# Graph passes with seven and ten row buffers, three one-hot buffers, and table rows stored bank by bank

## The chip, the core and the metric

The kernel runs on one core of one Trainium2 chip. The metric is the device time of one execution in microseconds (us); of the kernel before there are three timed runs and one profiled execution. The engines are TensorE (PE; its weight loads are listed as PEld), VectorE (DVE), ScalarE (ACT), GpSimd (POOL) and SyncE (SP), which only issues transfers.

## What is computed

Four graph layers over 3125 nodes with 256 features and 53125 edges, each followed by a layer norm: a filter layer, an attention layer, a three-step mean aggregation, and two relational convolutions. The change touches the last two. Cut to what matters:

```python
# layer 3 (L2): three times
agg = segment_sum(h[src], dst) / deg
h = relu(agg @ W_agg[l] + h @ W_self[l] + b_hid[l])
# then h @ W_out + b_out, residual and layer norm
# layer 4 (L3): two convolutions with relu between
xb  = einsum('ni,bio->nbo', x, basis)            # 4 bases
msg = einsum('eb,ebo->eo', comp[edge_type], xb[src])
agg = segment_sum(msg * norm[key][:, None], dst)
out = agg + x @ root + bias
```

## The kernel before

The edges were sorted at the start of the kernel. They lie in NT = 440 tiles of 128 edges; four tiles (U = 4) are a **group**, so that a pass has 110 groups. The nodes are NB = 25 blocks of 128. A **pass** goes over all edges once:

- GpSimd gathers, for each tile, 128 rows of 1 KB from a table in HBM into a row buffer (`rows`). It does so with one indirect transfer per tile, four per group, and before it reuses a buffer it waits on the semaphore `summed`, until the group that had the buffer has been summed.
- VectorE builds the one-hot matrices of a group (`hot`, 128x512), one operation, or two where edges have weights.
- TensorE multiplies one-hot by rows (each f32 product stands in the profile as two matmuls of 128x256, so a group is eight) and adds into one of four PSUM banks, one increment of `summed` for each tile. It waits for the rows (`gathered`) and for `hotted`.
- ScalarE fills a bank for a block (`fill`) and drains it (L1491) when the block's last tile is summed.

There are five passes. Four are made by `fused_pass`: two of the mean aggregation that also make the next table with 256 columns (the first and the second pass here), a third that has a projection and a layer norm in between (`measure`) and makes a table with 8 x 256 = 2048 columns, `rel_table`, and a fourth that makes the second `rel_table`. The fifth is made by `aggregate_pass`, which only sums. The code of `fused_pass` is straight line: the class `Posts` says after which group a finished block is turned (TensorE transposes, L1437; VectorE copies, `keep`, L1517) and, one group later, multiplied by the next layer's weights (`product`, L1451; VectorE takes the result out of PSUM in `take`, L1551, one copy for each 512-column bank plus one for the part that stays in SBUF). VectorE works in order: at step n it makes the one-hot of group n + 2 (AHEAD = 2), and then what `Posts` asks for after group n.

All buffers are rings. `g.RING` = 5 is the number of row buffers and of one-hot buffers in all five passes. The rows of the next table stand in two buffers `o` of all the columns; SP stores a buffer with one transfer when all its banks have been taken, and VectorE waits in `take` for the store of two blocks before (`stored`).

The two waits on which the passes turn are, on GpSimd and on VectorE:

```python
if n >= ring:
    pool.wait_ge(summed, (n - ring + 1) * U + 1)     # L1415, L1248
...
if n >= ring:
    dve.wait_ge(summed, (n - ring + 1) * U + 1)      # L1504
```

Between two passes all engines meet at a barrier, after the last store has landed.

## Time and profile before

| | us |
|---|---|
| median of three timed runs | 8323.25 (8320.33 to 8326.89) |
| the profiled execution's own time | 8298.08 |
| its span, first to last instruction | 8296.4 |
| first pass, 4961 to 5604 | 643 |
| second pass, 5604 to 6246 | 642 |
| third pass (with projection), 6246 to 6957 | 711 |
| fourth pass, 6957 to 7627 | 670 |
| fifth pass (sums only), 7627 to 8262 | 635 |

The five passes are 3301 us of the span. Everything before 4961 us is as it was, and so is what comes behind the fifth pass.

How to read it: an engine's busy time is a share of its stretch. "Idle" before an instruction is put down to whatever released it last by the profile; where the named one is a transfer that had ended long before (here "DMA table<-p_o" or "DMA bias<-bias_parts"), the wait belongs to another semaphore of the same instruction. "issue" is idle time for which the profile shows no wait. On GpSimd an idle time of 0.30 us before each gather is the rule.

### The profile page before, as it was taken

What the parts mean: (1) busy time and instruction counts of PE and PEld (TensorE: products, weight loads), DVE (VectorE), ACT (ScalarE), POOL (GpSimd) and SP (SyncE); (2) the same over time, 40 slices, a digit from 0 to 9 for tenths busy, and PEclk for the clock granted to TensorE, in tenths of its full rate; (3) what the DMA queues carried; (4) which work ended last, traced back from release to release, by engine and by line L of the source; (5) the groups of instructions that cost most, each with busy time, mean ns of one, the idle gap of its engine ahead of it and who ended that gap; (6) DMA issues with size and microseconds to landing.
All of it is one profiled execution on the core that took longest, in us unless ns stands there. A gap on an engine that the chain in (4) does not pass through costs nothing. (4 is left out here: it accounts for less than half of the span.)

```text
span 8296.4 us, 76731 instructions
## 1 busy us (share of the span) xinstructions
PE 5016.2 (60%) x19899; PEld 3266.6 (39%) x19900; DVE 3362.9 (41%) x7405; ACT 1335.8 (16%) x3186; POOL 4680.3 (56%) x4578
## 2 busy tenths in 40 slices
PE   1675754726633555555688885555556786776554
PEld 1342432414422333333465764433434454444333
DVE  8335346302212666666788432111213443333222
ACT  0332321300212222222222540000000000000000
POOL 3565754662364666566344216666665664665765
PEclk7786876857766565566799997776777887888666
DMA  2232321215204555455343013333333333444333
GB/s 81 83 99 67 99 81 58 90 42 170 96 22 129 165 161 162 151 160 161 116 121 109 14 36 97 98 92 104 99 97 106 129 128 102 131 129 114 94 91 89
DMA packets 413034, 865.48 MB, mean 104 GB/s; under 512 B 87540, under 2 KB 248707, under 8 KB 406326
## 3 DMA queue, kind: packets, MB, share of 16 engines
q0 software_dynamic: 216368, 576.59, 24.0%
q1 hardware_dynamic: 196486, 286.70, 10.3%
q8 instruction: 87, 1.43, 0.1%
q14 instruction: 93, 0.76, 0.0%
HBM read 664.47 MB, written 198.58 MB: 104 GB/s over the span
## 5 line engine op out<-in xcount | busy, mean ns | idle before, releaser
L1419 POOL DMA_INDIRECT p_rows<-table,idx_s x1320 | 1282.9, 972 | 776.8 <-issue 372.1
L1463 PE MATMUL p_psA<-p_rows,p_hot 128*128 128x256 f32 x3520 | 1044.6, 454 | 556.1 <-DMA p_rows<-table,idx_s 219.9
L1463 PEld LDWEIGHTS p_psA<-p_rows,p_hot 128*128 128x128 f32 x3520 | 779.6, 229 | 772.9 <-issue 644.8
L1768 DVE TENSOR_REDUCE p_best<-p_psM 128x8 f32<-128x1024 f32 x440 | 537.3, 1221 | 541.5 <-remote 351.8
L520 POOL DMA_INDIRECT rec_s<-p_space,p_row_s x416 | 452.5, 1088 | 519.8 <-DVE p_space L717 400.0
L1667 POOL DMA_INDIRECT p_kg<-kv_table,p_at x440 | 455.9, 1036 | 465.2 <-ACT p_at L1631 346.0
L1684 PE MATMUL p_psM<-ident,p_cold 128*128 128x512 bf16 x880 | 417.6, 573 | 378.1 <-DVE p_best L1768 259.5
L755 POOL DMA_INDIRECT rec_d<-edge_d,norm x416 | 399.7, 961 | 401.3 <-POOLq L76 271.9
L592 PE MATMUL p_psW<-p_wf,p_hid 128*128 128x256 f32 x1664 | 596.1, 492 | 0.0
L1419 POOL DMA_INDIRECT p_rows<-rel_table,edge_d x440 | 431.8, 981 | 267.7 <-issue 123.8
L512 POOL DMA_INDIRECT p_space<-h_table,at_d x416 | 442.3, 1063 | 209.0 <-issue 126.5
L1252 POOL DMA_INDIRECT p_rows<-rel_table,edge_d x440 | 439.9, 1000 | 210.6 <-issue 126.7
L1551 DVE COPY p_o<-p_psO 128x512 f32<-128x512 f32 (+1 forms) x250 | 158.1, 638 | 958.0 <-remote 497.9
L1667 POOL DMA_INDIRECT p_qg<-q_table,p_at x440 | 440.0, 1000 | 140.4 <-issue 140.4
L1267 PE MATMUL p_psA<-p_rows,p_hot 128*128 128x256 f32 x880 | 344.4, 553 | 288.7 <-DMA p_rows<-rel_table,edge_d 215.7
L1687 PEld LDWEIGHTS p_psM<-p_splitT,choose 96*128 96x128 bf16 x3520 | 371.5, 138 | 214.7 <-issue 194.5
L717 DVE SCALAR_TENSOR_TENSOR p_space<-p_psW,p_space 128x256 f32<-128x256 f32 x416 | 172.6, 477 | 697.4 <-remote 325.3
L1687 PE MATMUL p_psM<-p_splitT,choose 96*128 96x128 bf16 x3520 | 417.3, 290 | 0.0
L592 PEld LDWEIGHTS p_psW<-p_wf,p_hid 128*128 128x128 f32 x1664 | 350.7, 234 | 103.5 <-issue 30.4
L1852 POOL TENSOR_TENSOR p_val<-p_val 128x1024 f32<-128x1024 f32 x110 | 210.3, 1911 | 318.2 <-ACT p_val L1841 314.6
L1267 PEld LDWEIGHTS p_psA<-p_rows,p_hot 128*128 128x128 f32 x880 | 226.2, 272 | 407.1 <-issue 368.2
L805 PE MATMUL p_psA<-p_msg,p_hot 128*128 128x257 f32 x880 | 244.6, 418 | 211.4 <-issue 197.0
(316 smaller groups left out, 8252.7 us busy)
## 6 DMA issues: line engine op xcount, KB each, us to landing
p_msg<-rec_s SPq DMA_DIRECT2D x110, 520.0 KB
v_sorted<-p_kg SPq DMA_DIRECT2D x110, 512.0 KB
p_val<-v_sorted SPq DMA_DIRECT2D x110, 512.0 KB
rel_table<-p_o SPq DMA_DIRECT2D x50, 1024.0 KB
p_rows<-table,idx_s POOLq DMA_INDIRECT x1320
p_rows<-rel_table,edge_d POOLq DMA_INDIRECT x880
p_att<-edge_attr SPq DMA_DIRECT2D x104, 127.0 KB
table<-p_o SPq DMA_DIRECT2D x75, 128.0 KB
```

The lines of the kernel that those rows point to most:

```text
L512: pool.indirect_dma_start(msg[q][:, u, 0:D], None, table, bass.IndirectOffsetOnAxis(ap=g.at_d[:, n * U + u:n * U + u + 1], axis=0))\
L520: pool.indirect_dma_start(g.rec_s_rows, bass.IndirectOffsetOnAxis(ap=row_s[:, n * U + u:n * U + u + 1], axis=0), msg[q][:, u, :], None).th ...
L592: step = pe.matmul(psW[:, u, :], hid[t.q % few][:, k, u * P:(u + 1) * P], wf2[:, k, :], start=False, stop=(k == KT - 1))
L755: pool.indirect_dma_start(g.rec_d_rows, bass.IndirectOffsetOnAxis(ap=g.row_d[:, j:j + 1], axis=0), g.rec_all[:, j, :], None).then_inc(plac ...
L1252: pool.indirect_dma_start(rows[q][:, u, :], None, table, bass.IndirectOffsetOnAxis(ap=idx(n * U + u), axis=0))\
L1267: pe.matmul(psA[:, bass.ds(step[u], D)], hot[t.q][:, u, :], rows[t.q][:, u, :], start=False, stop=True, skip_group_check=True).then_inc(su ...
L1419: pool.indirect_dma_start(rows[q][:, u, :], None, table, bass.IndirectOffsetOnAxis(ap=idx(n * U + u), axis=0))\
L1463: pe.matmul(psA[:, bass.ds(step[u], D)], hot[q][:, u, :], rows[q][:, u, :], start=False, stop=True, skip_group_check=True).then_inc(summed, 1)
L1667: pool.indirect_dma_start(rows[t.q][:, u, :], None, table, bass.IndirectOffsetOnAxis(ap=at[t.q][:, u, n:n + 1], axis=0))\
L1684: pe.matmul(psM[u % 2][:, h:h + 4, :].rearrange("p h e -> p (h e)"), cold[t.q][:, u, :], g.ident4[:, :], start=True, stop=False)
L1687: step = pe.matmul(psM[u % 2][:, h, :], choose[:, u * H + h, :], splitT[t.q][:, :], start=False, stop=(h % 4 == 3))
L1768: dve.tensor_reduce(best[:, u, :], psM[u % 2][:, :, :], X, ALU.max).then_inc(found[u], 1)
```

## The change

It has three parts.

1. The number of row buffers is 7 in the four fused passes (`g.ROWS`) and 10 in the fifth (`g.LASTS`), where it was 5.
2. The number of one-hot buffers is 3 in the fused passes (`g.HOTS`); it stays 5 in the fifth.
3. The rows of the next table go through four buffers of one bank each (512 columns, or 256 in the first two passes) and not through two of all columns. SP stores each bank when it has been taken, and VectorE waits before each bank for the store of four banks ago.

```diff
 def aggregate_pass(...)
-    NT, NB, groups, ring = g.NT, g.NB, g.NT // U, g.RING
+    NT, NB, groups, ring = g.NT, g.NB, g.NT // U, g.LASTS
+    hots = g.RING
...
-        hot = [s.sb(f"hot{q}", [P, U, P]) for q in range(ring)]
+        hot = [s.sb(f"hot{q}", [P, U, P]) for q in range(hots)]
...
-                    wait(dve, summed, after(t, ring))
+                    wait(dve, summed, after(t, hots))
...
 class Spread
+        self.sent = [bank[0][0:2] for bank in self.banks if not bank[0][2]]
...
 def fused_pass(...)
-    NT, NB, groups, ring = g.NT, g.NB, g.NT // U, g.RING
-    AHEAD, TURNS, OUTS, OUTB = 2, 3, 2, 3
+    NT, NB, groups, ring, hots = g.NT, g.NB, g.NT // U, g.ROWS, g.HOTS
+    AHEAD, TURNS, OUTS, OUTB = 2, 3, 4, 3
...
-        o = [s.sb(f"o{q}", [P, spread.cols]) for q in range(OUTS)]
+        o = [s.sb(f"o{q}", [P, min(BANK, spread.cols)]) for q in range(OUTS)]
...
-                    sp.wait_ge(taken, posts.made[Posts.SPREAD, k])
-                    sp.dma_start(spread.table[bass.ds(b * P, P), :], o[k % OUTS][:, :]).then_inc(stored[k % OUTS], 16)
+                    for j, (c0, c1) in enumerate(spread.sent):
+                        i = k * len(spread.sent) + j
+                        sp.wait_ge(taken, posts.made[Posts.SPREAD, k] - len(spread.banks) + j + 1)
+                        sp.dma_start(spread.table[bass.ds(b * P, P), c0:c1], o[i % OUTS][:, :]).then_inc(stored[i % OUTS], 16)
...
-                    q, c = n % ring, slice(n * U, (n + 1) * U)
-                    if n >= ring:
-                        dve.wait_ge(summed, (n - ring + 1) * U + 1)
+                    q, c = n % hots, slice(n * U, (n + 1) * U)
+                    if n >= hots:
+                        dve.wait_ge(summed, (n - hots + 1) * U + 1)
...
-                    if k >= OUTS:
-                        dve.wait_ge(stored[k % OUTS], 16 * (k // OUTS))
                     for j, bank in enumerate(spread.banks):
                         last = posts.made[Posts.SPREAD, k] - len(spread.banks) + j
+                        i = k * len(spread.sent) + j
+                        if i >= OUTS and j < len(spread.sent):
+                            dve.wait_ge(stored[i % OUTS], 16 * (i // OUTS))
...
-    g.RING = 5
+    g.RING, g.ROWS, g.HOTS, g.LASTS = 5, 7, 3, 10
```

The order of the work on TensorE, ScalarE and GpSimd stays. On SP, the stores of two blocks of the third pass were these; `rel_table0` is the table that the pass makes, `o0` and `o1` are the two buffers of all columns, and the loads of `order_s` fetch the block's number:

```order
L1408 ISA
L1408 DMA rel_table0<-p17_o0 128x2048
L159 TENSOR_LOAD order_s
L1408 ISA
L1408 DMA rel_table0<-p17_o1 128x2048
```

and the stores of one block are now these:

```order
L1413 ISA
L1413 DMA rel_table0<-p17_o0 128x512
L1413 ISA
L1413 DMA rel_table0<-p17_o1 128x512
L1413 ISA
L1413 DMA rel_table0<-p17_o2 128x512
L1413 ISA
L1413 DMA rel_table0<-p17_o3 128x512
```

One transfer of 1024 KB behind one wait has become four of 256 KB, each behind a wait of its own (the rows named ISA).

On GpSimd, the gathers of the fifth pass went over five buffers. Here is where it comes back to the first of them; a name in brackets is that of a semaphore's first user, and both names stand for `summed` here:

```order
L1252 DMA p19_rows3<-rel_table1,edge_d 128x256 x4
L1252 DMA p19_rows4<-rel_table1,edge_d 128x256 x4
L1252 DMA p19_rows0<-rel_table1,edge_d 128x256 [waits p1_filled]
L1252 DMA p19_rows0<-rel_table1,edge_d 128x256 x3
L1252 DMA p19_rows1<-rel_table1,edge_d 128x256 [waits p1_filled]
```

The same place is now:

```order
L1253 DMA p19_rows7<-rel_table1,edge_d 128x256 x4
L1253 DMA p19_rows8<-rel_table1,edge_d 128x256 x4
L1253 DMA p19_rows9<-rel_table1,edge_d 128x256 x4
L1253 DMA p19_rows0<-rel_table1,edge_d 128x256 [waits p1_bias_in]
L1253 DMA p19_rows0<-rel_table1,edge_d 128x256 x3
```

GpSimd's first wait on `summed` moves from the sixth group to the eleventh, and in each later group it asks for the sums of ten groups before, not of five.

## Rows read from the trace of the kernel before

**Rows 1.** The five passes by window: length, busy time by engine, clock, DMA.

```profile
core 0: us, PE busy (x) PEld busy (x) DVE busy (x) ACT busy (x) POOL busy (x), PEclk, DMA share, GB/s
4961.00:5604.00 643.00, 348.94 (x1159) 255.86 (x1159) 118.17 (x217) 23.58 (x50) 428.01 (x440) 0.76 0.35 98
...
6246.00:6957.00 711.00, 542.45 (x1636) 337.30 (x1637) 272.48 (x786) 23.54 (x50) 426.18 (x441) 0.84 0.38 119
6957.00:7627.00 670.00, 468.60 (x1460) 290.05 (x1459) 232.56 (x371) 19.27 (x50) 431.77 (x440) 0.84 0.42 126
7627.00:8262.00 635.00, 345.68 (x883) 226.36 (x881) 147.90 (x220) 19.02 (x50) 439.91 (x440) 0.71 0.33 91
```

**Rows 2.** GpSimd's waits in the first pass: us in total, times, longest.

```profile
POOL p_rows L1419 <- issue: 124.6, 407, 0.6
...
POOL p_rows L1419 <- DMA table<-p_o: 51.1, 16, 5.3
POOL p_rows L1419 <- PE p_psA L1463: 18.0, 16, 4.7
```

**Rows 3.** The same in the fifth pass.

```profile
POOL p_rows L1252 <- issue: 126.7, 416, 0.3
POOL p_rows L1252 <- PE p_psA L1267: 42.6, 20, 5.4
...
POOL p_rows L1252 <- DMA table<-p_o: 14.6, 3, 5.2
```

**Rows 4.** Fifth pass, GpSimd in order of time: start, us, idle before.

```profile
7774.77 1.40 POOL L1252 DMA_INDIRECT p_rows<-rel_table,edge_d  x1 [4.86 <-DMA table<-p_o]
...
7819.95 0.94 POOL L1252 DMA_INDIRECT p_rows<-rel_table,edge_d  x1 [0.30 <-issue]
7826.04 1.41 POOL L1252 DMA_INDIRECT p_rows<-rel_table,edge_d  x1 [5.15 <-DMA table<-p_o]
```

**Rows 5.** Fifth pass, the same stretch, TensorE's sums of single groups.

```profile
7792.64 1.99 PE L1267 MATMUL p_psA<-p_rows,p_hot 128*128 128x256 f32 x8 [1.22 <-DMA p_rows<-rel_table,edge_d]
7797.69 3.42 PE L1267 MATMUL p_psA<-p_rows,p_hot 128*128 128x256 f32 x8 [3.06 <-DMA p_rows<-rel_table,edge_d]
7802.74 1.99 PE L1267 MATMUL p_psA<-p_rows,p_hot 128*128 128x256 f32 x8 [1.63 <-DMA p_rows<-rel_table,edge_d]
```

**Rows 6.** Fifth pass, the same stretch, VectorE's one-hots.

```profile
7794.80 0.69 DVE L1295 TENSOR_TENSOR p_hot<-iota,edge_d 128x512 f32<-128x512 f32 x1 [1.68 <-PE p_psA L1267]
...
7809.12 0.69 DVE L1295 TENSOR_TENSOR p_hot<-iota,edge_d 128x512 f32<-128x512 f32 x1 [12.80 <-issue]
...
7825.93 0.69 DVE L1295 TENSOR_TENSOR p_hot<-iota,edge_d 128x512 f32<-128x512 f32 x1 [15.27 <-DMA table<-p_o]
```

**Rows 7.** First pass, all engines around one stop.

```profile
5108.28 2.01 PE L1451 MATMUL p_psO<-w_hid,p_xT 128*128 128x256 f32 x4
...
5121.93 0.95 POOL L1419 DMA_INDIRECT p_rows<-table,idx_s  x1 [0.30 <-issue]
5126.24 0.42 DVE L1551 COPY p_o<-p_psO 128x256 f32<-128x256 f32 x1 [18.68 <-remote]
5126.57 0.94 POOL L1419 DMA_INDIRECT p_rows<-table,idx_s  x1 [3.70 <-DMA table<-p_o]
...
5126.91 2.49 DVE L1505 TENSOR_TENSOR p_hot<-iota,loc_s 128x512 f32<-128x512 f32 x4
5127.78 4.63 PE L1463 MATMUL p_psA<-p_rows,p_hot 128*128 128x256 f32 x10 [13.23 <-DVE p_hot L1505]
```

**Rows 8.** Fourth pass, all engines around its first stop.

```profile
6991.55 0.38 PE L1437 MATMUL p_psT<-ident,sums 128*128 128x128 f32 x2
...
7006.80 0.94 POOL L1419 DMA_INDIRECT p_rows<-rel_table,edge_d  x1 [0.30 <-issue]
7013.35 0.42 DVE L1517 COPY p_xT<-p_psT 128x256 f32<-128x256 f32 x1 [34.53 <-DMA bias<-bias_parts]
...
7013.55 0.94 POOL L1419 DMA_INDIRECT p_rows<-rel_table,edge_d  x1 [5.80 <-DMA table<-p_o]
...
7013.83 10.10 PE L1451 MATMUL p_psO<-big,p_xT 128*128 128x512 f32 x16 [16.50 <-DVE p_xT L1517]
```

**Rows 9.** Third pass, around one stop: TensorE's sums end as GpSimd goes on.

```profile
6426.34 3.62 PE L1463 MATMUL p_psA<-p_rows,p_hot 128*128 128x256 f32 x16
...
6428.51 0.94 POOL L1419 DMA_INDIRECT p_rows<-table,idx_s  x1 [4.30 <-PE p_psA L1463]
```

**Rows 10.** VectorE's waits in the fourth pass: us in total, times, longest.

```profile
DVE p_xT L1517 <- DMA bias<-bias_parts: 198.6, 15, 34.5
DVE p_o L1551 <- PE p_psO L1451: 116.5, 67, 7.5
```

**Rows 11.** SP's last stores of the fourth pass, and the fifth pass's first one-hot.

```profile
7607.78 13.70 SPq L1408 DMA_DIRECT2D rel_table<-p_o  x2
...
7626.39 0.69 DVE L1295 TENSOR_TENSOR p_hot<-iota,edge_d 128x512 f32<-128x512 f32 x1 [5.43 <-PEq L76]
```

More of the change, by code:

```diff
@@ L1266, in total @@
                     for u in range(U):
-                        pe.matmul(psA[:, bass.ds(step[u], D)], hot[t.q][:, u, :], rows[t.q][:, u, :],
+                        pe.matmul(psA[:, bass.ds(step[u], D)], hot[t.q % hots][:, u, :], rows[t.q][:, u, :],
                                   start=False, stop=True, skip_group_check=True).then_inc(summed, 1)
@@ L1293, in make_hot @@
                     c = bass.ds(t.n * U, U)
-                    wait(dve, summed, after(t, ring))
-                    dve.tensor_tensor(hot[t.q][:, :, :], bc(g.iota[:, :], 1, U), bc(loc[:, c], 2, P), ALU.is_equal)\
+                    wait(dve, summed, after(t, hots))
+                    dve.tensor_tensor(hot[t.q % hots][:, :, :], bc(g.iota[:, :], 1, U), bc(loc[:, c], 2, P), ALU.is_equal)\
                         .then_inc(marked, 1)
                     dve.wait_ge(marked, t.n + 1)
-                    dve.tensor_tensor(hot[t.q][:, :, :], hot[t.q][:, :, :], bc(weight[:, c], 2, P), ALU.mult).then_inc(hotted, 1)
+                    dve.tensor_tensor(hot[t.q % hots][:, :, :], hot[t.q % hots][:, :, :], bc(weight[:, c], 2, P), ALU.mult).then_inc(hotted, 1)
                 pipelined(dve, groups, ring, [(0, make_hot)])
@@ L1379, in fused_pass @@
         rows = [s.sb(f"rows{q}", [P, U, D]) for q in range(ring)]
-        hot = [s.sb(f"hot{q}", [P, U, P]) for q in range(ring)]
+        hot = [s.sb(f"hot{q}", [P, U, P]) for q in range(hots)]
         xT = [s.sb(f"xT{q}", [P, KT, P]) for q in range(TURNS)]
-        o = [s.sb(f"o{q}", [P, spread.cols]) for q in range(OUTS)]
+        o = [s.sb(f"o{q}", [P, min(BANK, spread.cols)]) for q in range(OUTS)]
         stats, bits, part_f = s.sb("stats", [P, 6]), s.sb("bits", [P, 1], I32), s.sb("part", [P, 1])
@@ L1406, in _ @@
                     b = block_of_rank(core.nc, g, plan, SPE, k)
-                    sp.wait_ge(taken, posts.made[Posts.SPREAD, k])
-                    sp.dma_start(spread.table[bass.ds(b * P, P), :], o[k % OUTS][:, :]).then_inc(stored[k % OUTS], 16)
+                    for j, (c0, c1) in enumerate(spread.sent):
+                        i = k * len(spread.sent) + j
+                        sp.wait_ge(taken, posts.made[Posts.SPREAD, k] - len(spread.banks) + j + 1)
+                        sp.dma_start(spread.table[bass.ds(b * P, P), c0:c1], o[i % OUTS][:, :]).then_inc(stored[i % OUTS], 16)
                 for q in range(OUTS):
-                    sp.wait_ge(stored[q], 16 * len(range(q, NB, OUTS)))
+                    sp.wait_ge(stored[q], 16 * len(range(q, NB * len(spread.sent), OUTS)))
             @block.gpsimd
@@ L1462, in _ @@
                         for u in range(U):
-                            pe.matmul(psA[:, bass.ds(step[u], D)], hot[q][:, u, :], rows[q][:, u, :],
+                            pe.matmul(psA[:, bass.ds(step[u], D)], hot[n % hots][:, u, :], rows[q][:, u, :],
                                       start=False, stop=True, skip_group_check=True).then_inc(summed, 1)
@@ L1543, in take @@
                         flat(own)[:, bass.ds(block_of_rank(core.nc, g, plan, DVE, k) * D, D)]
-                    if k >= OUTS:
-                        dve.wait_ge(stored[k % OUTS], 16 * (k // OUTS))
                     for j, bank in enumerate(spread.banks):
                         last = posts.made[Posts.SPREAD, k] - len(spread.banks) + j
+                        i = k * len(spread.sent) + j
+                        if i >= OUTS and j < len(spread.sent):
+                            dve.wait_ge(stored[i % OUTS], 16 * (i // OUTS))
                         dve.wait_ge(made, last + 1)
                         for c0, c1, biased in bank:
-                            out = own_term if biased else o[k % OUTS][:, c0:c1]
+                            out = own_term if biased else o[i % OUTS][:, :]
                             step = dve.tensor_copy(out, psO[last % OUTB][:, c0 - bank[0][0]:c1 - bank[0][0]])
```

## The prediction, as put on record before the changed kernel ran

> **What bounds the kernel now.** I read the passes by window first [rows 1]. No engine is full in any of them, and GpSimd is the nearest: 440 gathers of 0.95 us and more, each behind 0.30 us of idle time. That is 428 to 440 us of busy time plus 440 x 0.30 = 132 us, 560 to 572 us of work that nothing shortens in passes of 635 to 711 us. What lies above is stops. In the first pass GpSimd's waits on anything but "issue" are 51.1 + 18.0 us in 32 times [rows 2]; less the ordinary 0.30 us each, 59.5 us. In the fifth they are 42.6 + 14.6 in 23 times [rows 3], 50.3 us.
>
> What are the stops? In the fifth pass GpSimd issues without a break from 7774.77 to 7820.89 (7819.95 + 0.94) and then stands for 5.15 us [rows 4]. That run is 36 gathers, nine groups. The group that it asks for at 7826.04 is five groups back, and TensorE had summed it in the 1.99 us from 7802.74 [rows 5]: 21 us earlier. The buffer had long been free; the news was late. VectorE shows the same. The one-hot at 7794.80 starts 0.17 us behind the sum that it waits for (7792.64 + 1.99 = 7794.63), 20 us into GpSimd's run. The next one waits for the sum that ended at 7801.11 and comes at 7809.12, 8 us late; the one behind it waits for the sum that ended at 7804.73 and comes at 7825.93, 0.11 us before GpSimd goes on [rows 5, 6]. So TensorE's increments arrive at once for some 20 us of uninterrupted gathers, then they trickle (one group in about 14 us, while GpSimd uses one in 5), and all that is owed arrives some 5 us behind GpSimd's last gather. The first pass has it too: a product ended at 5110.29, VectorE takes it at 5126.24, and GpSimd had been silent since 5122.88 [rows 7]. In the fourth pass a transpose that ended at 6991.93 is copied at 7013.35, 0.2 us before GpSimd goes on after 5.80 us [rows 8]. I call this the late state. What makes it the trace does not say; that it ends with GpSimd's silence is what every one of these rows shows.
>
> The third pass is different. There GpSimd's stop at 6428.51 ends 0.3 us behind a true sum (of the sixteen products from 6426.34 the first half ends, at an even pace, at 6426.34 + 3.62 / 2 = 6428.15) [rows 9], and TensorE is busy for 542 of 711 us. TensorE and VectorE hold that pass, not the buffers. The fourth lies between: TensorE 469 us busy, and VectorE waits 198.6 us in 15 times for transposes [rows 10]; 469 + 199 = 668 of 670 us.
>
> **The change part by part.** The sum is made against the profiled execution (8298.08 us) and laid on the median of 8323.25, 25 us (0.3%) above it.
>
> *Ten row buffers in the fifth pass.* GpSimd can run 5 groups further before it has to ask for a late sum, 20 gathers x 1.25 = 25 us. The distance of two stops was 7826.04 - 7774.77 = 51.3 us, twelve of them in 635 us; now it would be 76 us, eight. Four stops fewer at 4.85 (5.15 less 0.30) are 19 us. Against it: VectorE keeps its five one-hot buffers and still gets no news, so TensorE stops after five groups and up to five more wait filled. If the pass ends in such a state, these cost 1.99 to 3.77 us each behind the last gather, 0 to 17 us; I take 3 on the mean. Net -16, bounds -25 and 0.
>
> *Seven row buffers in the first two passes.* A stop costs 3.4 us (3.70 less 0.30) and there are about 59.5 / 3.5 = 17 a pass, one in 37 us. Two groups more are 10 us: one in 47, 3.5 stops fewer, 12 us a pass. But TensorE must make up more at each stop: VectorE, held at a copy, had let it do only two groups [rows 7], now five wait where three did. It works off a group in some 3 us (349 us / 110) while GpSimd adds one in 5, so it gains 2 us in 5 and needs about 15 us more of the 20 timely ones. The late state then starts with a backlog and the ring fills sooner. I take a third, -4 a pass, -8 for both; bounds -12 and +3 each.
>
> *Seven row buffers in the third and fourth pass.* Here the longer run works against the pass. What TensorE and VectorE wait for ends when GpSimd falls silent, and it falls silent two groups, 10 us, later. In the steady state that cancels: a TensorE that is the slower one lets GpSimd fill the ring whatever its size, and the time from the start of the late state to the full ring does not depend on it. At the start it does not cancel: the first late copy (7013.35) would come at about 7023 [rows 8]. I take +6 for each; bounds 0 and +10 for the third, -10 and +20 for the fourth, whose stops (stated below) are partly of the first kind.
>
> *Three one-hot buffers in the fused passes.* VectorE now asks before the one-hot of group n + 2 for the sums of group n - 1, where it asked for n - 3. Behind this wait stand the copies of finished blocks, for which TensorE waits. But at the same step those copies wait for TensorE's work after group n, which lies behind group n - 1. In the late state VectorE stands already at such a copy, with two groups of one-hots made. I take 0; bounds 0 and +5 a pass. In return no more than three one-hots come in a row after a stop, against four in 2.49 us [rows 7].
>
> *Stores bank by bank.* The bytes are the same. SP issues 100 transfers for 25 in the third and fourth pass, and nothing else is queued there. VectorE's waits on `stored` rise from 23 to 96 a pass; the buffer that each asks for was sent a block, 26 us, before, and the whole store with the barrier fits in the 4.9 us between the last issue (7621.48) and the next pass's first one-hot (7626.39) [rows 11]. So none of them holds; an instruction more costs nothing where four one-hots with their waits take 2.49 us, and at most 0.06 us: 0 to +9 for 146, I take +1. What is gained is the end of each of these passes, where the last 256 KB go out alone and not 1024 KB: a part of those 4.9 us, I take 1.5 each, -3, bounds -5 and 0.
>
> The DMA share of these passes is 0.38 and 0.42 [rows 1]. The Trainium skill ("DMA: Bandwidth & Descriptors", Rules for kernel authors) asks for 1 MiB and more in one transfer for full bandwidth, which speaks against the split. It would matter if the transfers bound the pass; by these shares they don't, and by the page's rule as by the rows the sum stays.
>
> Sum: -16 - 8 + 6 + 6 + 1 - 3 = -14 us. Forecast 8323 - 14 = 8309 us.
>
> **The rivals.**
>
> *The stops go away.* The late state might pass by itself if only GpSimd can run on. For it: between 7809.12 and 7825.93 nobody asked for a group whose sum was older than 21 us, so that no row says what a longer run would bring. Against it: in that run the increments of one group arrived in 14 us and the next not in 17. Price: the 59.5 us of the first pass [rows 2], as much for the second, which is built alike, and 50.3 for the fifth [rows 3], 169 us: 8154; if it holds for the fifth pass alone, 8323 - 50 + 8 = 8281, and half of all of it 8239. The Trainium skill ("Perfetto Trace Analysis", Optimization Strategy) says that a gap which repeats on the engine that should be saturated can mean too few buffers; here the gap repeats, but the buffer it waits for was free 21 us before [rows 4, 5].
>
> *Longer silence is paid in the fourth pass (slower).* VectorE's 15 waits for transposes [rows 10] end where GpSimd stops. If the ring's two groups are added not to the first of them but to every second, 7 x 10 = 70 us are added, and the stops saved in that pass give back at most 20: +50; with the third pass's few late waits +10, and the gains of the other passes -24, the whole is about +36: 8359. The point from which it decides is TensorE's backlog: it decides if TensorE has caught up by the time the late state starts, since then the two groups more are waited for in full. With every fourth wait the result is 8335.
>
> *It does nothing that can be measured.* The stops move and their sum stays, because each is set by what TensorE has left: 8323, within 8 us.
>
> **How the numbers follow.** A measurement of this kernel tells about 0.2%, 16.6 us, from no change. Forecast: chance 0.55, 8309 with 8285 to 8325 around it, of which half lies under 8306.6. Stops go away, wholly or in part: 0.15, faster. Slower: 0.18, nearly all of it over 8340. Nothing: 0.12, nearly all within. So faster 0.28 + 0.15 + 0.01 = 0.44; same 0.27 + 0.01 + 0.10 = 0.38; slower 0.18. The forecast's unknown terms reach from -60 to +40 if all go one way; the range 8235 to 8345 takes in its own and the part of each rival that is next to it, and leaves out about 0.08 below and 0.10 above. For the likeliest case alone it is 8285 to 8325.
>
> **What would show it.** In the profile after: the fifth pass with about eight stops of 5 us, some 76 us apart, 40 to 45 us of waits that are not "issue" for 57, and VectorE's one-hots late by up to 45 us just before each. The first two passes with 13 to 16 stops each. In the fourth, the first transpose after 6991 copied 30 us late and not 21, and the sum of VectorE's waits for transposes at 199 us or a little more. The third pass within 10 us of 711. No copy out of PSUM that waits for a store. I would be wrong if runs of GpSimd well over 80 us without a stop appear, or if the stops are as many as before; and the sizes are wrong, though not the steps, if TensorE's backlog behind the last gather of the fifth pass is over 15 us.

## The result

Beside each other in one job, the changed kernel took 8357.69 us (median of 7 runs, 8325.14 to 8372.43) and the kernel before 8320.33 (7 runs): a ratio of 1.005, 95% interval 1.0028 to 1.0072. It is slower, where 14 us less was forecast. A second job with both gave 8333.61 against 8304.44, ratio 1.0039 (1.0022 to 1.0055).

The profiled execution after has a span of 8370.7 us, 74 over the one before; it is the slowest of its seven, and the one before (8298.08) was among the faster ones, so that the 74 us overstate the 37 between the medians. Here are its five passes by window, with the columns of [rows 1]:

```profile
4989.00:5632.00 643.00, 334.63 (x1159) 254.38 (x1157) 120.67 (x217) 23.62 (x50) 434.41 (x440) 0.74 0.35 98
5632.00:6278.00 646.00, 325.71 (x1160) 248.78 (x1161) 121.15 (x218) 23.56 (x50) 431.63 (x440) 0.73 0.35 98
6278.00:7017.00 739.00, 554.92 (x1638) 346.49 (x1636) 272.22 (x786) 23.55 (x50) 425.15 (x441) 0.83 0.38 114
7017.00:7701.00 684.00, 464.12 (x1458) 290.17 (x1457) 235.78 (x370) 19.30 (x50) 441.53 (x440) 0.83 0.43 123
7701.00:8337.00 636.00, 323.19 (x884) 212.86 (x884) 147.97 (x220) 19.05 (x50) 440.10 (x440) 0.66 0.34 91
```

The first, second and fifth pass are as long as before, within 4 us. The third took 28 us more, the fourth 14 by these windows. Another 28 us lie ahead of the first pass (it starts at 4989 and not at 4961), where the program is the same.

**What the fifth pass does.** GpSimd in order of time, from one stop to the next, as in [rows 4]:

```profile
7893.98 1.40 POOL L1253 DMA_INDIRECT p_rows<-rel_table,edge_d  x1 [6.11 <-PE p_psA L1268]
...
7986.86 0.95 POOL L1253 DMA_INDIRECT p_rows<-rel_table,edge_d  x1 [0.30 <-issue]
7996.30 1.41 POOL L1253 DMA_INDIRECT p_rows<-rel_table,edge_d  x1 [8.49 <-PE p_psA L1268]
```

This run is 72 gathers, twice the 36 of [rows 4]. But the stop behind it is 8.49 us, not 5.15. A run with its stop took 51.3 us for 36 gathers before, 102.3 for 72 after: 1.42 us a gather both times. All in all the stops (idle times of over 0.7 us) were 13 with 54 us, and are 7 with 52.

TensorE is worse off than before. In the long run it stands between single matmuls of one group, even between the two halves of one product, where it waits for nothing that the program names. What holds it there no run shows; e6_after_one_inc, below, has the same gaps with a quarter of the increments.

```profile
7855.87 0.59 PE L1268 MATMUL p_psA<-p_rows,p_hot 128*128 128x256 f32 x1 [0.59 <-issue]
7858.67 0.59 PE L1268 MATMUL p_psA<-p_rows,p_hot 128*128 128x256 f32 x1 [2.21 <-issue]
7862.17 0.58 PE L1268 MATMUL p_psA<-p_rows,p_hot 128*128 128x256 f32 x1 [2.91 <-issue]
7865.67 0.59 PE L1268 MATMUL p_psA<-p_rows,p_hot 128*128 128x256 f32 x1 [2.92 <-issue]
```

Gaps of over 1.2 us inside a group occur 48 times in this pass, 100 us in all; there was none before. They cost nothing: the last sum ends 10.8 us behind GpSimd's last gather, and 10.6 before.

**Where the third pass loses.** All three engines at its start, in order of time for each (TensorE, VectorE, GpSimd):

```profile
6300.11 3.12 PE L1468 MATMUL p_psA<-p_rows,p_hot 128*128 128x256 f32 x8 [3.01 <-DMA p_rows<-table,idx_s]
...
6310.08 3.77 PE L1468 MATMUL p_psA<-p_rows,p_hot 128*128 128x256 f32 x8 [1.18 <-DMA p_rows<-table,idx_s]
...
6326.29 3.77 PE L1468 MATMUL p_psA<-p_rows,p_hot 128*128 128x256 f32 x8 [12.01 <-issue]
```

```profile
6303.67 0.69 DVE L1510 TENSOR_TENSOR p_hot<-iota,loc_s 128x512 f32<-128x512 f32 x1 [9.02 <-PE p_psA L1468]
6325.38 0.69 DVE L1510 TENSOR_TENSOR p_hot<-iota,loc_s 128x512 f32<-128x512 f32 x1 [21.01 <-remote]
6339.38 0.69 DVE L1510 TENSOR_TENSOR p_hot<-iota,loc_s 128x512 f32<-128x512 f32 x1 [13.31 <-remote]
```

```profile
6332.20 0.95 POOL L1424 DMA_INDIRECT p_rows<-table,idx_s  x1 [0.31 <-issue]
6339.61 1.28 POOL L1424 DMA_INDIRECT p_rows<-table,idx_s  x1 [6.46 <-remote]
```

The one-hot at 6325.38 is that of the seventh group. With three buffers it needs the sums of the fourth, which ended at 6300.11 + 3.12 = 6303.23; the news is 22 us late, and the next, for the fifth group, 30. TensorE sums the sixth group at 6310.08 and stands 12 us for the next one-hot. With five buffers the one-hots of groups seven and eight were made before the late news mattered. The sums of group eight end 67.8 us into the pass, 50.9 before: 17 us are lost there and then. At the 26th group the difference is 18 us, at the last 31. GpSimd's ring of seven is full only at 6332.20 + 0.95 = 6333.15, 55 us into the pass (with five it was at 40).

### The profile page after: what moved, and what is told of

Read it like the earlier page. It is cut to its first block and busy times, and to the rows that moved or that the text cites. A ratio compares the mean times of both kernels' runs of the same rounds, so it can differ in the third digit from the quotient of the medians.

```text
span 8370.7 us, 77223 instructions
## 1 busy us (share of the span) xinstructions
PE 4971.6 (59%) x19899; PEld 3255.4 (39%) x19900; DVE 3370.7 (40%) x7405; ACT 1336.4 (16%) x3186; POOL 4689.1 (56%) x4578
## 5 line engine op out<-in xcount | busy, mean ns | idle before, releaser
L1468 PE MATMUL p_psA<-p_rows,p_hot 128*128 128x256 f32 x3520 | 1010.3, 445 | 583.2 <-issue 404.6
L1468 PEld LDWEIGHTS p_psA<-p_rows,p_hot 128*128 128x128 f32 x3520 | 775.2, 226 | 768.2 <-issue 641.7
L1268 PE MATMUL p_psA<-p_rows,p_hot 128*128 128x256 f32 x880 | 321.3, 512 | 311.5 <-issue 189.1
L1510 DVE TENSOR_TENSOR p_hot<-iota,loc_s 128x512 f32<-128x512 f32 x330 | 223.2, 686 | 463.7 <-remote 273.1
L1268 PEld LDWEIGHTS p_psA<-p_rows,p_hot 128*128 128x128 f32 x880 | 212.5, 253 | 420.8 <-issue 390.5
```

The costliest lines, as they stand in the source:

```text
L1268: pe.matmul(psA[:, bass.ds(step[u], D)], hot[t.q % hots][:, u, :], rows[t.q][:, u, :], start=False, stop=True, skip_group_check=True).then ...
L1468: pe.matmul(psA[:, bass.ds(step[u], D)], hot[n % hots][:, u, :], rows[q][:, u, :], start=False, stop=True, skip_group_check=True).then_inc ...
```

## The experiments

The jobs came in two kinds, which has to be known to read them. In three jobs the median of the kernel before was 8304 to 8320 us, in five 7073 to 7080. One chip number (8) appears in both kinds, so the number does not tell them apart, and what makes the one or the other no record here shows. I call them **jobs of 8300** (all that was known when predicting) and **jobs of 7080**; the expectations that speak of two kinds of chips mean these. A ratio is always against the kernel before in the same job. The passes below are measured from the first gather of one to the first gather of the next, the fifth to its last sum; "long" counts gathers of over 1.05 us in the fourth and the fifth pass:

```
run                  kind  ahead   1st    2nd    3rd    4th    5th    long 4th/5th
before               8300  4961.8  643.0  641.9  710.3  670.0  634.4  42/86
after                8300  4989.5  643.2  645.8  738.5  684.7  634.1  68/85
e7_after_again       8300  4965.6  643.6  644.2  730.4  666.2  633.2  61/81
e6_after_one_inc     8300  4974.4  646.6  642.9  725.3  669.1  632.9  62/86
g1_one_step_hot      8300  4960.6  643.8  642.7  707.3  656.1  633.7   2/0
g2_after_one_step    8300  4969.3  643.6  647.2  723.0  683.3  637.7   1/0
e1_last10            7080  4069.0  579.9  581.2  637.8  589.4  577.4  33/53
e3_hots3             7080  4065.5  584.6  583.0  635.0  604.9  578.9  85/54
e4_banks             7080  4066.6  580.5  580.5  635.2  585.5  581.0  31/60
e5_one_inc           7080  4068.5  581.5  581.0  631.5  590.3  580.4  31/56
f1_hots5_34          7080  4063.1  583.5  581.2  636.0  588.4  582.0  34/62
f2_rows5_34          7080  4073.3  587.4  583.4  635.8  602.1  577.6  91/49
h2_banks_one_step    7080  4061.3  578.4  581.5  635.5  574.8  562.1   0/1
```

**e1_last10** (the kernel before): ten row buffers in the fifth pass, nothing else.

```
-    NT, NB, groups, ring = g.NT, g.NB, g.NT // U, g.RING
+    NT, NB, groups, ring = g.NT, g.NB, g.NT // U, g.LASTS
```

> Only the fifth pass changes: ten row buffers for five, the rest is the kernel before. Theory A, formed on the profile after: TensorE's increments and GpSimd's gathers share something that gives out one gather per about 1.42 us on the mean, so a longer run of gathers is paid by a longer stop (8.9 us for 4.9). The fifth pass stays at 635 us within 3, with about seven stops of 8 to 9 us, and the whole within 5 us of before. Theory B, the prediction: a stop costs 5 us however long the run before it was; in another run than the one profiled the fifth pass would be 616 to 622 us and the whole 14 to 19 us under before.

7069.69 us, ratio 1.0001 (0.9992 to 1.001): nothing. But in a job of 7080 GpSimd has no stop at all that the ring could remove. Its waits in the fifth pass, us in total, times, longest:

```profile
POOL p_rows L1253 <- issue: 125.5, 412, 0.3
...
POOL p_rows L1253 <- PE p_psA L1268: 8.2, 27, 0.3
```

What such a job is shows in the windows of the first, third, fourth and fifth pass:

```profile
4069.00:4649.00 580.00, 364.00 (x1160) 260.03 (x1159) 118.54 (x217) 23.61 (x50) 426.41 (x441) 0.80 0.38 109
5230.00:5868.00 638.00, 509.19 (x1636) 321.26 (x1635) 275.31 (x786) 23.57 (x50) 427.50 (x441) 0.89 0.43 133
5868.00:6457.00 589.00, 471.05 (x1459) 299.15 (x1458) 232.73 (x371) 19.30 (x50) 429.01 (x440) 0.88 0.48 143
6457.00:7035.00 578.00, 337.07 (x884) 229.08 (x882) 152.17 (x220) 18.74 (x50) 433.62 (x440) 0.70 0.37 100
```

GpSimd's gathers are as long as in [rows 1], and each pass but the third is 440 x (0.97 + 0.30) us and a short tail. The third pass is 72 us shorter than in a job of 8300, the fourth 81, the first 63. No profile of a job of 7080 has a stop in the first, second, fourth or fifth pass. So the late state, which the prediction took for a property of this program, appears in some jobs and not in others. The run tells nothing between the theories on the ring; the fifth passes of the jobs of 8300 do (634.4 and 633.7 us with a ring of five, 634.1, 633.2, 632.9 and 637.7 with ten).

**e3_hots3**: three one-hot buffers in the first four passes, rows and stores of before.

```
-    NT, NB, groups, ring = g.NT, g.NB, g.NT // U, g.RING
+    NT, NB, groups, ring, hots = g.NT, g.NB, g.NT // U, g.RING, 3
```

> Only the one-hot buffers of the first four passes go from five to three; rows and stores are those of before. Theory A: the three one-hot buffers make the third and fourth passes slower, since VectorE waits longer in front of its copies: third pass +15 to +28 us, fourth +10 to +15, the whole +20 to +40 us. Theory B: they cost nothing (0 to +5 a pass, as predicted), and the 28 and 15 us of these passes come from the seven row buffers or the stores: the whole within 8 us of before.

7088.65 us, ratio 1.0022 (1.0013 to 1.0031): 16 us, which is the fourth pass, 604.9 us where the other kernels of that job have 585.5 to 590.3. No pass has more waits. The third and the fourth pass by window:

```profile
5233.00:5868.00 635.00, 510.63 (x1636) 322.22 (x1635) 277.07 (x786) 23.54 (x50) 426.24 (x440) 0.89 0.43 133
5868.00:6473.00 605.00, 470.94 (x1461) 299.20 (x1460) 237.93 (x371) 19.27 (x50) 443.83 (x440) 0.88 0.46 139
```

GpSimd is busy 443.8 us in the fourth pass and 429.0 in that of e1_last10: the 440 gathers themselves are 15 us longer. This is how (VectorE and GpSimd in order of time, fourth pass):

```profile
6053.47 0.68 DVE L1508 TENSOR_TENSOR p_hot<-iota,edge_d 128x512 f32<-128x512 f32 x1
6053.56 1.41 POOL L1422 DMA_INDIRECT p_rows<-rel_table,edge_d  x1 [0.30 <-issue]
...
6054.18 0.69 DVE L1512 TENSOR_TENSOR p_hot<-p_hot,norm 128x512 f32<-128x512 f32 x1
6054.85 0.69 DVE L1508 TENSOR_TENSOR p_hot<-iota,edge_d 128x512 f32<-128x512 f32 x1
6055.27 1.09 POOL L1422 DMA_INDIRECT p_rows<-rel_table,edge_d  x1 [0.30 <-issue]
6055.58 0.69 DVE L1512 TENSOR_TENSOR p_hot<-p_hot,norm 128x512 f32<-128x512 f32 x1
...
6058.39 0.95 POOL L1422 DMA_INDIRECT p_rows<-rel_table,edge_d  x1 [0.30 <-issue]
```

The three gathers beside VectorE's compare (L1508) and multiply (L1512) take 1.09 to 1.42 us, one beside nothing 0.95. Each gather of over 1.05 us of the fourth pass overlaps a multiply: 85 of 85 here, 33 of 33 in e1_last10, and 42 of 42 in the kernel before. Not each gather beside a multiply is long: 37 here and 88 in e1_last10 are not. With three one-hot buffers VectorE makes the one-hots in other places, and 85 gathers are hit where 33 were.

The compare does it too. The first three passes have no multiply, and yet 27 to 56 long gathers each in every profile; most of them lie beside the compare, which also takes two tensors. In the third pass of the kernel before these are 35 of 35, and here is one (VectorE and GpSimd in order of time):

```profile
6412.73 0.67 DVE L1505 TENSOR_TENSOR p_hot<-iota,loc_s 128x512 f32<-128x512 f32 x1
6413.00 1.22 POOL L1419 DMA_INDIRECT p_rows<-table,idx_s  x1 [0.30 <-issue]
...
6414.53 0.94 POOL L1419 DMA_INDIRECT p_rows<-table,idx_s  x1 [0.30 <-issue]
```

**e4_banks**: the stores bank by bank alone (`OUTS` = 4, `sent`), rings of before.

> Only the stores change: four buffers of one bank, stored one by one, in the first four passes. Prediction's terms: +1 for the waits and -3 for the tails, the whole within 5 us of before. Rival: the stores themselves (100 issues for 25 in the third and fourth pass, with as many more waits on VectorE) are what made these passes slower: third +28, fourth +15, the whole +30 to +43 us.

7066.22 us, ratio 0.999 (0.9981 to 0.9999): 7 us less, where the prediction's two terms make 2. In the profiles the third and fourth pass are 3 and 4 us shorter than in e1_last10. The rival, that the stores cost, is out where nothing is late; in a job of 8300 it wasn't tried alone.

**e5_one_inc** (the kernel before) and **e6_after_one_inc** (the changed one): TensorE counts a group and not its four tiles.

```
-                            pe.matmul(...).then_inc(summed, 1)
+                            last = pe.matmul(...)
+                        last.then_inc(summed, U)
```

> The kernel before, with one increment of the sums' semaphore for a group of four tiles, by 4, where there were four by 1, in all five passes. Nothing else changes. Theory A: TensorE's increments have to get past GpSimd's gathers, each at a price of about 0.17 us of GpSimd's time (1.42 less 1.25), so that three quarters of the stops go in the first, second and fifth pass: about 45 us each, 120 to 170 us in all, 8150 to 8200 us. Theory B: the gathers themselves can be served only one in 1.42 us, whatever TensorE reports; the three passes stay at 643, 642 and 636 us within 4, and the coarser news costs 0 to 10 us in the third and fourth.

> The changed kernel with one increment of the sums' semaphore for a group of four tiles, by 4, where there were four by 1. On a chip without the late news: within 5 us of the changed kernel by either theory. On a chip with it (the kernel before at some 8320 us): theory A, TensorE's increments are what has to get past the gathers, 100 us and more under the changed kernel, the fifth pass at 590 us and under; theory B, the gathers are served one in 1.42 us whatever TensorE reports, within 10 us of the changed kernel, the fifth pass at 635 us.

e5_one_inc ran in a job of 7080: 7070.95 us, 1.0002 (0.9993 to 1.0011), which leaves its question open. e6_after_one_inc got a job of 8300: 8330.12 us against 8333.61 of e7_after_again beside it, the fifth pass 632.9 us against 633.2. A quarter of TensorE's increments of these sums, and the pass is the same to 0.3 us; TensorE stands inside groups as before (44 times, 89 us). The number of increments is not what costs; theory A as it stands there falls, and the times are those of theory B.

**e7_after_again**: the whole change once more.

> The whole change once more, beside the kernel before on the chip that runs it. In the runs of the parts the kernel before took 7073 us, its gathers had no stop in the first, second, fourth and fifth pass, and only the three one-hot buffers cost anything (16 us, all in the fourth pass). Theory A: on a chip like that one the change is the sum of its parts, +8 to +18 us, with the fourth pass at about 604 us and the others at 581, 581, 635 and 580. On a chip where the kernel before takes some 8320 us it is +30 to +45 us, with the third and fourth pass 15 to 30 us longer and the first, second and fifth as before. Theory B: the seven row buffers, which no part had alone, cost by themselves: over +25 us on either chip.

It got a job of 8300: +29 us, where 30 to 45 was expected. Against the profile before (of another job), its third pass has +20, the fourth -4, the others are within 3. The fourth pass gave 15 us more in one profile and 4 less in the other; the third gave 28 and 20, and 15 in e6_after_one_inc.

**f1_hots5_34** and **f2_rows5_34**: the change with five one-hot buffers, or with five row buffers, in the third and fourth pass.

```
+    if spread.cols > D:
+        hots = 5          # f2_rows5_34: ring = 5
```

> The whole change, but with five one-hot buffers again in the third and fourth pass. Theory A: the three one-hot buffers are what costs there (e3_hots3 lost 16 us in the fourth pass). On a chip where before takes 8300 us: third pass 708 to 715 us for 730, fourth 665 to 670, the whole within 10 us of before; on one where it takes 7073: fourth pass 586 to 590, the whole within 8 us of before. Theory B: the seven row buffers cost in the third pass, since VectorE's and TensorE's late news is released by GpSimd's stops and these come two groups later: on an 8300 us chip the third pass stays at 725 to 740 and the whole at +20 us or more; on a 7073 us chip there is no late news and nothing is left (0).

> The whole change, but with five row buffers again in the third and fourth pass (three one-hot buffers stay). Theory A (the one-hots cost): third pass at 725 to 740 us on an 8300 us chip, the whole +20 us or more; on a 7073 us chip the fourth pass at 604 and the whole +10 to +16. Theory B (the rows cost): third pass at 708 to 715, the whole within 10 us of before, on an 8300 us chip; on a 7073 us chip as by theory A.

Both in a job of 7080: 7076.52 (0.9996, 0.9988 to 1.0005) and 7095.23 us (1.002, 1.0011 to 1.0029). The fourth pass is 588.4 us with five one-hot buffers and seven row buffers, 602.1 with three and five, with 34 and 91 long gathers. There, the one-hot buffers are all that costs, and seven row buffers in these two passes neither cost nor bring anything that can be seen. The kernel of f1_hots5_34 ran three times more, to see it in a job of 8300 (h1, i1 and j1_hots5_34), and each job was one of 7080: ratios 0.9997, 0.9992 and 0.9995.

**f4_paced** and **i2_paced_more**: the kernel before, with GpSimd slowed in the fifth pass.

```
+                        pool.wait_ge(padded, n * U + u)
+                        pool.memset(pad[:, :], 0.0).then_inc(padded, 1)
```

> The kernel before, in whose fifth pass GpSimd writes a scratch buffer of 128x128 behind each gather (0.2 us in the rows of before, perhaps 0.05 more with its wait), so that it issues a gather in 1.45 to 1.55 us and not in 1.25. Theory A: on a chip where before takes 8300 us, gathers are served at one in 1.42 us, and what the engine runs ahead of that comes back as stops and late increments. Then the stops go away with the pace: the fifth pass takes 440 x 1.45 to 1.55 + 12 = 650 to 695 us with no stop over 1 us, and TensorE's sums are taken within 0.3 us. Theory B: the late news has nothing to do with the pace; the stops stay at some 50 us and come on top: 700 us and more. On a 7073 us chip both say 580 + 88 to 130 us.

> The kernel before, in whose fifth pass GpSimd writes a scratch buffer of 128x256 behind each gather. One of 128x128 took the pass from 581 to 624 us on a 7080 us chip, 1.40 us a gather, a little under 1.42; this one should take 1.45 to 1.52 us a gather. Theory A, a rate of one gather in 1.42 us: the pass takes 650 to 685 us on every chip, and on an 8300 us chip no stop over 1 us is left, TensorE does not stand between two matmuls of a group, and VectorE takes the sums within 0.3 us. Theory B, the late increments have nothing to do with the pace: on an 8300 us chip 50 us of stops stay on top, 700 us and more.

Jobs of 7080 all (i2_paced_more twice, the second as j2_paced_more): the pass took 624 us, and 661 and 658 with the longer write. This shows only that the pass there follows GpSimd's pace. Whether a pace of over 1.42 us would end the late increments in a job of 8300 was not seen.

**f3_half_rows**: gathers of half the bytes in the fifth pass.

> The kernel before, in whose fifth pass each gather fetches rows of 512 bytes, not 1024 (from the table seen as rows of half the length; TensorE multiplies the half rows twice, so that its work is the same). The other half of the rows is left out of the sums. Theory A: what serves one gather in 1.42 us is limited by bytes (91 GB/s in this pass): on a chip where before takes 8300 us the stops go away and the fifth pass takes 440 x 1.27 + 15 = 575 to 585 us. Theory B: it is limited by the number of gathers or of their 128 rows: the pass stays at 635 us within 5, with its 50 us of stops. On a 7073 us chip both say 580 us.

Again a job of 7080: the pass took 585.4 us, and 577 to 586 in the other runs of these jobs with whole rows. There, half the bytes make no gather shorter. What limits the gathers in a job of 8300 stays open.

**g1_one_step_hot** (the kernel before) and **g2_after_one_step** (the changed one): the weighted one-hots, those of the fourth and fifth pass, by one instruction a tile in place of a compare and a multiply of two tensors.

```
-                    dve.tensor_tensor(hot, iota, loc, ALU.is_equal).then_inc(marked, 1)
-                    dve.wait_ge(marked, t.n + 1)
-                    dve.tensor_tensor(hot, hot, weight, ALU.mult).then_inc(hotted, 1)
+                    for u in range(U):
+                        step = dve.tensor_scalar(hot[u], iota, loc[u], weight[u], ALU.is_equal, ALU.mult)
+                    step.then_inc(hotted, 1)
```

> The kernel before, whose weighted one-hots (fourth and fifth pass) are made in one step: four instructions of 128x128 that compare with the place and multiply by the weight, instead of a compare and a multiply of 128x512. Every gather over 1.05 us of these two passes lies beside such a multiply (33 of 440 in the fourth pass, 53 in the fifth, on a 7073 us chip). Theory A: these gathers are held by VectorE's multiply; without it there are under 10 of them a pass, the fourth pass is 6 to 9 us shorter, the fifth 12 to 17, the whole 18 to 26 us under before on a 7073 us chip; on an 8300 us chip, where gathers are served one in 1.42 us anyway, within 8 us. Theory B: the longer gathers only happen to lie there; 30 and more stay, the whole within 8 us of before on either.

> The whole change, with the weighted one-hots made in one step as in g1_one_step_hot. Theory A: what the three one-hot buffers cost in the fourth pass (15 us on a 7073 us chip; 85 to 91 long gathers for 33) is that the multiply falls on GpSimd's gathers more often; without the multiply this cost is gone: on a 7073 us chip the fourth pass is within 4 us of that of g1_one_step_hot, the whole within 6 us of it. Theory B: the cost is VectorE's or TensorE's waiting for buffers; the fourth pass stays 12 to 16 us above that of g1_one_step_hot. On an 8300 us chip: third pass 720 to 738 us by both, since its one-hots have no multiply, and the whole +15 to +30 over before.

A job of 8300: 8303.76 against 8317.86 us, ratio 0.9995 (0.998 to 1.0011), and 8358.17, ratio 1.0046 (1.0029 to 1.0063). The long gathers are gone in both. And here the rate shows best. The fifth pass of g1_one_step_hot by window, and GpSimd's waits in it:

```profile
7610.00:8245.00 635.00, 345.07 (x884) 234.00 (x882) 123.36 (x440) 19.05 (x50) 417.29 (x440) 0.70 0.34 91
```

```profile
POOL p_rows L1252 <- issue: 122.2, 400, 0.5
POOL p_rows L1252 <- PE p_psA L1267: 60.7, 28, 4.2
...
POOL p_rows L1252 <- DMA table<-p_o: 22.5, 11, 5.4
```

GpSimd is busy 417.3 us for 439.9 [rows 1], and its waits on anything but "issue" rose from 57 us [rows 3] to 83. What the gathers gave, the stops took: the pass is 633.7 us for 634.4. The fourth pass is 656.1 us for the 670.0 of before: from first gather to last it takes 1.43 us a gather and no longer 1.46, so there the shorter gathers did count.

g2_after_one_step has a third pass 16 us and a fourth 27 us longer than g1_one_step_hot beside it, though it has one long gather. So in a job of 8300 the long gathers are not what the change pays for. The first two waits at the start of its third pass are those of the profile after (VectorE, in order of time):

```profile
6286.14 0.69 DVE L1511 TENSOR_TENSOR p_hot<-iota,loc_s 128x512 f32<-128x512 f32 x1 [11.56 <-remote]
6308.54 0.69 DVE L1511 TENSOR_TENSOR p_hot<-iota,loc_s 128x512 f32<-128x512 f32 x1 [21.71 <-remote]
```

All four profiles of a changed kernel in jobs of 8300 have a one-hot there that waits 21.0 to 21.7 us and sums of the eighth group that end 67.8 to 68.6 us into the pass; the two with five one-hot and five row buffers have 50.9. In the fourth pass g2_after_one_step has 76.1 at this place and g1_one_step_hot 59.4: 17 us again. With the one-hots of the change as it was it is 6 us there, 76.0 after and 69.9 before.

**h2_banks_one_step**: the kernel before with the stores bank by bank and the one-step one-hots.

> The kernel before with the stores bank by bank and the weighted one-hots in one step; five row and five one-hot buffers. If VectorE's multiply is what lengthens the gathers: on a 7080 us chip the fourth pass at 578 to 582 us and the fifth at 562 to 568, the whole 22 to 32 us under before. If it is not: 4 to 8 us under, which is what the stores gave alone. On an 8300 us chip the third, first, second and fifth pass as before, the fourth 10 to 15 us shorter, the whole 10 to 20 us under before.

7032.15 us against 7074.11, ratio 0.9945 (0.9931 to 0.9958): the largest gain on record here. It ran in a job of 7080. Its gathers of the fourth and fifth pass in one row (us in all, mean ns), and below it those of e4_banks, which differs in the one-hots alone:

```profile
L1424 POOL DMA_INDIRECT p_rows<-rel_table,edge_d x440 | 417.5, 949 | 182.0 <-issue 121.0 <-POOLq L76 48.2 <-PE p_psA L1468 12.8
L1253 POOL DMA_INDIRECT p_rows<-rel_table,edge_d x440 | 417.4, 949 | 157.3 <-issue 126.8 <-SPq L1245 23.5 <-PE p_psA L1268 7.0
```

```profile
L1253 POOL DMA_INDIRECT p_rows<-rel_table,edge_d x440 | 435.9, 991 | 156.6 <-issue 124.3 <-SPq L1245 22.8 <-PE p_psA L1268 9.4
L1424 POOL DMA_INDIRECT p_rows<-rel_table,edge_d x440 | 428.8, 975 | 182.0 <-issue 123.1 <-POOLq L76 48.2 <-PE p_psA L1468 10.7
```

11 and 18.5 us of gathers are gone, and the passes are 10.7 and 18.9 us shorter. This settles the one-hots' part: in a job of 7080, where GpSimd bounds these two passes, VectorE's operations on two tensors lengthened them. The edit takes out the compare of two tensors together with the multiply, so it does not say how much was of either; and the first three passes, whose compare it leaves as it was, keep their 30 to 33 long gathers. The Trainium skill ("SBUF — State Buffer", SBUF: two separate sides) describes a port pair that VectorE and GpSimd lock against each other for a whole instruction; a VectorE operation with two inputs in SBUF meets there only a GpSimd operation that reads SBUF. The lengthening by up to 0.5 us beside compares and multiplies of 0.69 fits that if a gather counts as such a read, because it takes its indices from SBUF; no run here shows which part of the gather waits. The same page of the Trainium skill (Who interferes with whom) counts `tensor_scalar` among the operations that can take the pair too; here at most two gathers of 440 beside it were long.

## Right and wrong, step by step

**"A stop costs 5 us; four fewer are 19 us."** Wrong, and this was the main term (-16, and -8 for the first two passes). The step that failed is taking the price of a stop as fixed while making the run before it longer. Measured: 8.5 us after 72 gathers, 5.2 after 36. The passes of the jobs of 8300 have a rate, from the first gather to the last 1.41 to 1.42 us a gather in each of the first, second and fifth passes, with rings of five, seven and ten, with gathers of 0.95 or 1.00 us, with four increments a group or one. The warning stood in [rows 4]: 51.3 us over 36 gathers is the same 1.42 us as the whole pass, 624 us over 440, and as the first pass, 622 over 440. A quotient that passes with different work share, whatever the rings, looks like a rate, and buffers don't change a rate; what sets it is open. That the stops become fewer was right, but the term was mis-sized: the prediction let a run grow by 20 gathers, from 36 to 56, and gave about eight stops, 76 us apart. The runs doubled to 72, and there were seven, most of them 102 us apart, with 94 us of gathers between them. That is the prediction's own sign of being wrong, runs of well over 80 us. In exchange the one-hots of this pass start up to 50 us behind the end of the sum that they wait for, where it was 21 (it said up to 45).

**"Three one-hot buffers: 0 (0 to +5 a pass)."** Wrong. In a job of 7080 they alone cost 16 us, by longer gathers in the fourth pass, an overlap that the prediction does not have (e3_hots3). In a job of 8300 they are where the trace shows the first loss. The argument looked at the steady state, where VectorE stands at a copy anyway. It missed the start of a pass, where there is no finished block yet and the one-hots run ahead freely: there the wait is for sums of three groups before in place of five, and the first late news hits it. 17 us in the third pass. Whether the one-hot buffers do it alone, or only with a GpSimd that falls silent 15 us later because it has seven row buffers, isn't settled: no run in a job of 8300 had one without the other, nor the stores without both. The trace shows that the missing one-hot is what TensorE waits for. That the longer ring puts off the release fits the times (silent 55 us into the pass for 40), but is argued, not shown.

**"Seven row buffers in the third and fourth pass: +6 and +6."** Not tested by themselves in a job of 8300; in jobs of 7080 they cost nothing (f1_hots5_34). All changes together, against the profile before, gave +28, +20, +15 and +13 in the third (after, e7, e6, g2), and +15, -4, -1 and +13 in the fourth: a loss in the third each time, and no one sign in the fourth. The row on which the fourth rested, a transpose copied 21 us late [rows 8], matters less: VectorE's waits for transposes in the fourth pass fell from 218 to 78 us in all, and those for one-hots rose from 19 to 185. The largest rows of the pass after (us in total, times, longest):

```profile
DVE p_hot L1510 <- remote: 98.8, 11, 20.3
DVE p_hot L1510 <- PE p_psA L1468: 70.6, 32, 9.2
DVE p_xT L1522 <- remote: 57.0, 7, 12.6
```

**"Stores: +1 and -3."** Right in sign, if a little better: -7 in a job of 7080. In a job of 8300 they weren't tried alone.

**The rivals.** "The stops go away" didn't happen in any job of 8300. The rival on the slower side gave 8359 us, within 2 us of the median, but not by its mechanism: it wanted +50 in the fourth pass from waits for transposes, and there were +15 and -4, with most of the loss in the third. The number is a coincidence. That the job decides whether there is a late state at all was not among the cases; it would have made the first, second and fifth pass 57 to 63 us shorter by itself.

**The range.** The prediction says that its unknown terms reach from -60 to +40 if all go one way. Its own bounds add up to -64 and +65 (0 for the fifth pass, +6 for the first two, +10 and +20 for the third and fourth, +20 for the one-hots, +9 for the waits on stores), so the +37 that came lay inside them; the upper end of the range, 8345, is 22 us over the median and left a part of its own terms out. Two prices of rivals do not come out of its terms either: for the stops gone in the fifth pass alone they give 8323 - 50 + 2 = 8275 and not 8281, and with every fourth wait for a transpose (35 us in place of 70) about 8324 and not 8335. Neither bears on the forecast.

**The part ahead of the passes.** The profiles of changed kernels (after, e7, e6, g2) have +28, +4, +13 and +8 us there, g1_one_step_hot -1. The code is the same, and seven runs of the kernel before in one job spread over 34 us as a whole; where the 28 us come from stays open.

## What to carry to other kernels

Before a buffer is bought to remove stops, divide: length of the pass by number of transfers, and length of one run plus its stop by the transfers in it. If the two agree and other passes give the same number, the stops may be how a rate shows itself; then a deeper ring makes them fewer and longer, as here. Count the buffers of the other inputs, too, at the start of a pass and not only in its steady state: the ring that is cut for the one that grows may be what carried the pass through the first late message. And where GpSimd's gathers are the bound, look at what VectorE runs beside the longest of them.

## What the runs showed of the hardware

The same program takes 8304 to 8320 us in some jobs and 7073 to 7080 in others, under one chip number too. Between the profiles before and e1_last10 the difference is 893 us ahead of the passes and 63, 61, 72, 81 and 57 in the five; the stretch from 4067 to 4902 us, where nothing is gathered or scattered, is as long in either (835 and 839 us). In the slow kind the one-hots of the fifth pass start up to 21 us behind the sums that they wait for, and up to 50 with ten row buffers, where TensorE also stands 2.2 to 2.9 us between single matmuls. A gather takes 0.95 us alone and up to 1.47 beside VectorE's operations on two tensors, the compare as well as the multiply, and at most 1.06 in the passes whose one-hots are made by `tensor_scalar`. Halving its bytes doesn't shorten it in a job of 7080 (f3_half_rows).
